# Turning the probabilities before the late feed-forward products in a six-layer attention pipeline

## The reference

```python
for i in range(6):
    x = attn_layer(shift_tokens(x), Wqkv[i], q_scale[i], k_scale[i], Wo[i]) + x
    x = ffn_layer(shift_tokens(x), ln_g[i], ln_b[i], W1[i], b1[i], W2[i], b2[i]) + x
# attn_layer, 16 heads of 64, windows of 32 queries that see their own and the window before:
q, k, v = split(x @ Wqkv);  q = l2norm(q) * qs;  k = l2norm(k) * ksc      # then rotary, with scale
sim  = q . k * 8, masked;  attn = softmax(sim);  out = (attn @ v) @ Wo
# ffn_layer: layernorm, hg = xn @ W1 + b1, then (a * gelu(gate)) @ W2 + b2, inner width 341
```

## Time and profile before

| | |
|---|---|
| median of 3 runs | 5531.48 us (5512.16 to 5532.7) |
| the profiled execution | 5539.95 us, span 5538.1 us |
| PE, PE weight load busy | 5001.7 us (90%), 3294.1 us (59%) |
| DVE, ACT, POOL busy | 3943.2 us (71%), 3384.8 us (61%), 2857.0 us (52%) |
| chain that ended last | PE 73%, ACT 12%, issue 9%, DVE 2% |
| mean granted clock of TensorE | 0.954 |

### The profile page before, as it was taken

How to read it: one execution, slowest core, us unless ns; L and a number is a source line. 1 busy time by engine, 2 the same in 40 slices (tenths; PEclk the granted TensorE clock), 3 DMA queues, 4 the chain that set the end, 5 groups by cost and what they waited for, 6 DMA issues and landing times.

```text
span 5538.1 us, 170253 instructions
## 1 busy us (share of the span) xinstructions
PE 5001.7 (90%) x73888; PEld 3294.1 (59%) x74080; DVE 3943.2 (71%) x5095; ACT 3384.8 (61%) x5293; POOL 2857.0 (52%) x1423
## 2 busy tenths in 40 slices
PE   8899999999989999999999989985999899989999
PEld 5566666766666666666666666663222222256766
DVE  5888887777778888888888878853667767733333
ACT  2577777777767777777777767762455555541111
POOL 1877777777767777777777767741111111110000
PEclk8999999999999999999999999996799999979999
DMA  2111111111111111111111111113011111000000
GB/s 70 27 51 32 32 29 52 29 29 28 31 46 32 30 32 51 30 32 29 53 31 33 30 43 29 32 27 80 1 18 18 30 24 18 1 35 2 4 4 6
DMA packets 94969, 167.92 MB, mean 30 GB/s; under 512 B 24745, under 2 KB 36530, under 8 KB 92978
## 3 DMA queue, kind: packets, MB, share of 16 engines
q1 hardware_dynamic: 91378, 147.99, 9.8%
q10 hardware_dynamic: 2880, 9.44, 1.2%
HBM read 47.37 MB, written 10.49 MB: 10 GB/s over the span
## 4 chain that ended last, share of the span: by engine, by line
PE 73%; ACT 12%; issue 9%; DVE 2%; POOL 1%; SPq 1%; DMA 1%; ACTq 0%; DVEq 0%; POOLq 0%
PE D L1305 7%; PE D L1162 6%; PE D L1237 6%; PE D L1248 6%; PE D L1264 5%; PE D L1098 5%; PE D L1483 5%; PE D L1405 4%; PE D L1143 4%; PE D L1273 4%; PE D L1275 3%; PE D L1151 3%; ACT V L724 3%; PE D L1368 3%; PE D L1388 3%
## 5 line engine op out<-in xcount | busy, mean ns | idle before, releaser
L462 POOL TENSOR_TENSOR rn<-ss,mhalf 128x33 f32<-128x33 f32 (+2 forms) x198 | 1262.7, 6377 | 564.2 <-DVE ss L838 551.9
L973 DVE TENSOR_REDUCE mxp<-D 128x2 f32<-128x1024 f32 (+3 forms) x640 | 672.5, 1064 | 313.7 <-PE D L1372 154.3
L1305 PE MATMUL D<-PTb,V 64*64 64x32 f32 x24576 | 408.1, 220 | 202.7 <-ACT PTb L676 152.1
L724 ACT ACTIVATE V<-D 128x1024 f32<-128x1024 f32 (+3 forms) x426 | 366.1, 896 | 280.3 <-PE D L1388 279.0
L1305 PEld LDWEIGHTS D<-PTb,V 64*64 64x64 f32 x24576 | 389.0, 135 | 244.4 <-issue 244.1
L466 POOL TENSOR_TENSOR hh<-hh,rr 128x1024 f32<-128x1024 f32 x192 | 365.3, 1903 | 239.2 <-DVE rr L889 239.2
L941 DVE TENSOR_TENSOR TOK<-D,wA 128x1024 f32<-128x1024 f32 x384 | 466.5, 1215 | 0.0
L836 DVE TENSOR_REDUCE ss<-TOK 128x32 f32<-128x2048 f32 x192 | 437.2, 2277 | 0.0
L1216 PEld LDWEIGHTS D<-RK,w 128*128 128x128 f32 (+1 forms) x2304 | 274.0, 180 | 225.2 <-issue 221.3
L594 ACT ACTIVATE OTb<-D 128x1024 f32<-128x1024 f32 x192 | 197.0, 1026 | 331.8 <-PE D L1305 331.8
L1216 PE MATMUL D<-RK,w 128*128 128x128 f32 (+1 forms) x2304 | 327.6, 279 | 65.4 <-issue 62.1
(11 more groups left out here) (238 smaller groups left out, 11840.3 us busy)
## 6 DMA issues: line engine op xcount, KB each, us to landing
V<-V SPq DMA_DIRECT2D x936, 64.0 KB, 2.0
V<-V SPq DMA_DIRECT2D x192, 192.0 KB, 2.4
RB<-watt_dram SPq DMA_DIRECT2D x3, 2048.0 KB, 9.1
X<-watt_dram SPq DMA_DIRECT2D x3, 2048.0 KB, 9.1
parts_dram<-hh SPq DMA_DIRECT2D x48, 128.0 KB, 2.4
RA<-parts_dram SPq DMA_DIRECT2D x12, 384.0 KB
TOK<-parts_dram ACTq DMA_DIRECT2D x36, 128.0 KB
X<-parts_dram SPq DMA_DIRECT2D x12, 384.0 KB
```

The costliest lines, as they stand in the source:

```text
L462: pool.tensor_tensor(rn[:, st % 2, lo:hi], ss[:, st % 2, lo:hi], mhalf[:, lo:hi], ALU.pow).then_inc(s["powed"], 1)
L724: act.activation(PTE[i % 3][:, 2 * hp:2 * hp + 2, 0:CH - r * P], pair_of(("S", i + LAG, hp))[:, :].rearrange("p (h n) -> p h n", h=2)[:, : ...
L973: dve.tensor_reduce(mxp[:, 2 * hp:2 * hp + 2, qt, kc], pair_of(("F", at, hp))[:, :].rearrange("p (h n) -> p h n", h=2)[:, :, 0:keys], AX.X ...
L1305: m = pe.matmul(D01[64 * h:64 * h + 64, at:at + WIN], VW[g % 2][ks, (0 if r % 2 else 2) + h, p * DH:(p + 1) * DH], PTb[ks, p * P + 32 * r: ...
```

## The change

Seven edits:

1. On PE `turn_p(st - 1)` stands ahead of `ffn_late(st)`.
2. On ACT the two copies of turned probabilities stand right behind the V copies, ahead of the gelu part.
3. On DVE the late feed-forward part becomes `late_vector` and runs in the next step, behind the sum of squares and its floor.
4. All six straddling transfers wait for the value products of the block before (`pvdone` >= g instead of g - 1) and for both V copies.
5. The attention weights come in four transfers of 512 KB at blocks 10, 12, 14 and 16; the feed-forward weights with the fourth.
6. The residual comes back in four transfers at the same blocks of the last layer.
7. DVE's eight additions of the residual move from every fourth block to the last eight blocks.

```diff
             def straddling_windows(n):
...
-                if g < 2:
+                if g < 1:
                     sp.wait_ge(s["vw_zero"], 2)
                 else:
-                    sp.wait_ge(s["pvdone"], g - 1)
+                    sp.wait_ge(s["pvdone"], g)
+                sp.wait_ge(s["v_copied"], 2 * g + 2)
                 if n % BB:
                     sp.dma_start(v[0:32, 2, :], old[96:128, 0, :]).then_inc(arrived, 16)
                     sp.dma_start(v[64:96, 3, :], old[32:64, 1, :]).then_inc(arrived, 16)
-                sp.wait_ge(s["v_copied"], 2 * g + 1)
                 sp.dma_start(v[32:128, 2, :], v[0:96, 0, :]).then_inc(arrived, 16)
-                sp.wait_ge(s["v_copied"], 2 * g + 2)
...
-                if n % NB == 10 and n // NB + 1 < DEPTH:
-                    layer_weights(n // NB + 1)
-                elif n % NB == 10:
-                    sp.wait_ge(s["y_added"], (DEPTH - 1) * NB)
-                    sp.dma_start(XR[:, :], xkeep).then_inc(s["x_back"], 16)
+                if n % NB in (10, 12, 14, 16):
+                    l, piece = n // NB + 1, (n % NB - 10) // 2
+                    if l < DEPTH:
+                        layer_weights(l, piece)
+                    else:
+                        sp.wait_ge(s["y_added"], (DEPTH - 1) * NB)
+                        cols = slice(piece * 1024, piece * 1024 + 1024)
+                        sp.dma_start(XR[:, cols], xkeep[:, cols]).then_inc(s["x_back"], 16)
                 straddling_windows(n)
...
@@ att_scalar: the same seven lines stand behind the gelu part before @@
+                if 0 <= st - 1 < G:
+                    g = st - 1
+                    if g >= 1:
+                        act.wait_ge(s["pvdone"], g)
+                    for x in range(2):
+                        act.wait_ge(s["turnp"], 2 * g + x + 1)
+                        act.activation(PTb[:, x * CH:(x + 1) * CH], PB[6 + x], ACT.Copy).then_inc(s["pt_copied"], 1)
                 if ffn and st <= G + 4:
                     act.wait_ge(s["late3"], st - 1)
...
@@ att_vector @@
                     dve.tensor_scalar(sums, sums, 1e-24, None, ALU.max).then_inc(s["ss_ready"], 1)
+                late_vector(st - 1)
                 if 0 <= st + 1 < G:
...
-                    if b // NB == DEPTH - 1 and b % NBLK == NBLK - 1:
-                        c = b % NB // NBLK
+                    if b // NB == DEPTH - 1 and b % NB >= NB - NC:
+                        c = b % NB - (NB - NC)
                         dve.wait_ge(s["layer_out"], b + 1)
                         if c == 0:
-                            dve.wait_ge(s["x_back"], 16)
+                            dve.wait_ge(s["x_back"], 64)
...
+            def late_vector(st):
+
+                ffn = ffn_of(st)
                 if ffn and st <= G + 4:
                     dve.wait_ge(s["bank3_read"], st - 1)
...
@@ PE @@
+                if 0 <= st - 1 < G:
+                    turn_p(st - 1)
                 ffn_late(st)
                 if 0 <= st - 1 < G:
-                    turn_p(st - 1)
                     values(st - 1)
```

More of the change, by code:

```diff
@@ L333, in _, with layer_weights @@
             sp.dma_start(vecA[:, :], t["vecA"]).then_inc(s["wA_in"], 16)
-            def layer_weights(l):
+            def layer_weights(l, piece):
                 x = l % 2
[L338 to L351, removed]
+                cols = slice(piece * 1024, piece * 1024 + 1024)
+                if piece == 0:
+                    if l == 0:
+                        sp.wait_ge(s["gatedmul"], NC)
+                        sp.dma_start(RA[:, :], t["tabs"]).then_inc(s["tables_in"], 16)
+                    elif l == 1:
+                        sp.wait_ge(s["x_stored"], 16)
+                        sp.wait_ge(s["normed"], 3 * NC)
+                    else:
+                        sp.wait_ge(s["layer_out"], (l - 1) * NB)
+                        sp.wait_ge(s["tabs_ready"], (l - 1) * NB)
+                    sp.dma_start(QSB[x], t["qsb"][l].rearrange("p (a d) -> p a d", a=4)).then_inc(s[f"qsb_in{x}"], 16)
+                sp.dma_start(WB[x][:, cols], t["watt"][l][:, cols]).then_inc(s[f"attw_in{x}"], 16)
+                if piece == 3:
+                    sp.dma_start(W1S[x][:, :], t["W1"][l]).then_inc(s[f"ffw_in{x}"], 16)
+                    sp.dma_start(W2S[x][:, :, :], t["W2"][l]).then_inc(s[f"ffw_in{x}"], 16)
+                    sp.dma_start(FVS[x][:, :], t["fvec"][l]).then_inc(s[f"ffw_in{x}"], 16)
             def straddling_windows(n):
@@ L370, in straddling_windows @@
                 sp.dma_start(v[96:128, 3, :], v[64:96, 1, :]).then_inc(arrived, 16)
-            layer_weights(0)
+            for piece in range(4):
+                layer_weights(0, piece)
             sp.wait_ge(s["x1_ready"], NC)
@@ L669, in att_scalar @@
                     gelu(b, 1).then_inc(s["gelu"], 1)
[L670 to L676, removed]
                 if "spread" in ffn:
@@ L1225, in project_qk @@
                 if n == 0:
-                    pe.wait_ge(s[f"attw_in{l % 2}"], 16 * (l // 2 + 1))
+                    pe.wait_ge(s[f"attw_in{l % 2}"], 64 * (l // 2 + 1))
                 if l == 0:
```

## The result

The change takes 5302.0 us (median of 4 runs, 5299.3 to 5304.0) where the kernel before takes 5532.1 on the same chip: a ratio of 0.9575 on record, interval 0.9543 to 0.9607 (0.9584 by the two medians). Three of the four runs of the kernel before lie between 5512.2 and 5532.7; the fourth took 12960.8, which the median hardly feels.

A forecast was written before the change was run, and what follows sets the result against it. It took the step as bound by a ring through PE and ACT, closed at `values`, plus disturbed steps. 5539.95 - 53 (step) - 105 (stops) - 17.7 (residual) + 1 (additions) = 5365 us, range 5328 to 5450.

The forecast's parts named there:

- Two accounts, undisturbed period and stops: Six-layer pipeline: the undisturbed 17.78 us step can shorten; separately, disturbed steps lose 133 us (stops 114, residual wait 17.7).
- It ends at 17.46; I take 17.5: New step length set by ACT and DVE, against 17.78 us before: 53 us saved over 191 steps.
- The ring: Chain of waits through ACT and DVE, without PE, from L594 via exp and spread product back: 17.46 us worked out.
- Rival D: The ACT-DVE chain is shorter than worked out and PE's 17.0 us step binds: 5270 us, chance 0.02.
- Rival B: The chain of waits through ACT and DVE is longer, 17.9 us a step: 5441 us, chance 0.12.
- Bounds: all 114 saved, or none. I take 105.: PE's stops inside the value products and the slow steps after them: 105 us of 114 saved.
- Rival A: PE's stops inside the value products stay, price 105 us: about 5455 us, chance 0.10.
- The new wait of `project_out` for L600: Sign on PE: `project_out` waits about 0.3 to 0.5 us for ACT, replacing the wait before `values`.
- The residual: DVE's 17.70 us wait for the residual's return: 17.7 us saved, less 1 for additions moved to the end.
- The straddling transfers: Six transfers issued from the end of `values`, landing 5.6 us later: covered by 5 us before their first taker.
- The late part: DVE's late feed-forward part behind the sum of squares, the edit that costs: only 0.28 of 0.7 us a step arrives.
- Rival C, the clock: PE's clock falls in every step, with `values`, sixteen transposes and a wait in a row: 5753 us, chance 0.06.

The follow-up runs named there:

- experiments 2: The changed kernel with DVE's late feed-forward part back in its old place, at the end of its own step: 5257.0 us, ratio 0.9496.
- experiment 3: The changed kernel with ACT's affine instruction of the norm moved behind the exp of the next step: 5253.0 us, ratio 0.9486.
- experiment 10: The changed kernel, DVE's late part in its old place, plus a PE wait for ACT's first gelu attached to the first value product: 5389.3 us, ratio 0.9724.
- experiment 13: The kernel before with PE's wait for the turned probabilities named first, so attached to the first value product: 5387.8 us, ratio 0.9732.
- experiment 12: experiment 10 with the gelu wait named last, so that it stands alone as an instruction: 5553.0 us, ratio 1.0029.
- experiment 7: The kernel before with only DVE's late feed-forward part moved behind the sum of squares: 5638.1 us, ratio 1.0167.
- experiment 16: experiment 3 with PE's last eight late products placed in the middle of the value products: 5302.3 us, ratio 0.9573.

## Why the forecast was off, step by step

**Two accounts, undisturbed period and stops:** right. The steps took 235.1 us less. The period gives 191 x (17.78 - 17.29) = 94. Of the rest, 141, the stops and what follows them make 119, the residual 19 (one step of 36.7 us before), and the eleven steps at the two ends, which are mostly shorter than the period, 4. The working had called 114 and 17.7 "all of it". In fact the steps between the fifth and the 185th lost 122 us to stops and 19 to the residual, and short steps at the ends gave 7 back. What it left out are, among others, the stops in the transposes right behind `values` (L1143 and L1151, 14 with 11.1 us).

**"It ends at 17.46; I take 17.5".** This term was mis-sized; its mechanism was right. The ring has the members named and no others: L600 to the end of the exp 5.60, DVE to L916's end 0.03 + 8.37, L842 to L844 2.31 less 0.08, then 0.09 + 0.26 + 0.27, hand-over 0.04, L691 to L600 0.40; 17.29. I had taken an overlap of 0.09 at two joints. There are four: L842 behind L916, L941 behind L844, L600 behind L691, and one inside ACT's stretch to the exp (5.60, not 5.71). That is 191 x (17.5 - 17.29) = 40 of the 63 us by which the forecast missed, and enough to put it outside its range. Rival B, a longer ring, is out. Rival D is out for the change, and holds once the ring is opened: experiments 2 and 3 run at PE's own 16.94, where I had 17.0.

**"Bounds: all 114 saved, or none. I take 105."** The direction was right: all of the long stops but one in step 1 (2.0 us) and the clock steps behind them went. No run shows the 105 as a term; what the runs showed in its place is 119, another 14 of the 63. The stops that stay (7.6 us) lie in the ring's slack for the most part. The last 9 us of the miss are the residual, the ends and the profiled run being 2 us above the median. It is not the waiting itself that goes with the stops: PE waits for ACT ahead of `values` in 186 steps of experiment 10 (131.1 us in all) and in all 192 of experiment 13 (135.1 us), with one stop in each, and in 187 of experiment 12 (149.2 us), with 38. What differs between 10 and 12 is whether that wait is attached or stands in an instruction that only waits. In the change the last EVENT_SEMAPHORE ends 1.6 us ahead of the value products, and in the steps of the table the packet starts 0.1 to 2.1 us ahead of them; in the steps of the kernel before that stop it ends 0.06 ahead, and the packet starts 0.9 to 1.4 behind (5.6 at the longest stop). Rival A is out. The new wait of `project_out` for L600 is there, 49.9 us in 154 steps, in the trace attached to the first weight load of L1172, and PE has no "issue" idle time at that line.

**The residual** gave 19 against 17.7 less 1 for the additions. **The straddling transfers:** nothing, as said. **The late part** was called the edit that costs: 45 us, where the working had 0.42 x 191 = 80.

**Rival C, the clock:** out. Both windows read 1.00 with the value products, sixteen transposes and the short wait in a row, and with 24 transposes a step.

**Open:** why moving DVE's late part (experiment 7) makes steps with 103 to 112 products ahead of the boundary stop too, whose packet in the kernel before is mostly there in time; and why it comes late in a few of these there. The traces hold the times of packets, not of requests, so how a wait that stands alone and a late packet hang together is not shown; what is shown is that in every stopping step of the table's first row the packet starts after that wait's end, and that with the wait attached it starts ahead of the value products in all 45 steps of the table, in experiments 10 and 13 alike.

## What to carry to other kernels

If PE stops inside a run of small products with nothing to wait for, number its instructions: stops at a fixed place modulo 256 went with a late packet of q8 here (0.9 us or more behind the start of the value products at 28 of the 29 stops of the kernel before). Then look at the waits in front of the run, and name first the one that is met last, so that it is attached to the product; here that alone was worth 2.7%, without the reordering. When a bound is removed, work out the next ring to a tenth of a microsecond per joint, and open it before shipping: the change left 49 us (experiment 3) behind a ring that it had made itself.

## What the hardware showed that I had not expected

- With the wait that is met last standing alone (before, experiment 12), all 17 steps with 116 or more weight loads of `values` ahead of the boundary stopped, in each of the two; with it attached (experiments 13 and 10) none did. In the stopping steps of the kernel before it is 1.0 to 1.5 us, mostly 1.1, from the end of that wait's record to the packet's start (5.6 at the longest stop), and 2.2 to 2.6 from there to the first product behind the boundary.
- With the wait attached, PE also stood idle for less: 0.71 us for the same copy (experiment 13) where with it alone it was 0.81 (before), and the step is 17.68 where it was 17.78 (17.71 against 17.80 in experiments 10 and 12).
- The stop of 1.60 us in the earlier trace rows has more behind it: 6.8 us at clock 0.50, with eight transposes (L1143) at 1.97 us for 1.09.
- ACT's and DVE's next instruction often starts about 0.1 us before the row of the last one ends: in the change's step 0.08 to 0.09 at 12 joints of DVE and 0.09 to 0.12 at 9 joints of ACT. It doesn't behind DVE's reductions (L912 to L916 and L842 to L844, 0.04 after), nor around ACT's table loads and small copies of shifted tokens (0.01 to 0.02 after).
- Two more changes between full products and 64x64 tiles go with 0.33 us a step (17.27 in experiment 16, 16.94 in 3), about 0.16 each.
